# A fused transformer layer on one core: another order of the software-pipelined stages

## What is computed

```
patches: 13 x 13 cells, 11 x 11 of them -> emb = patches @ W.T + b + pos       (121 x 192)
h = concat([emb, txt])                                                          (249 x 192)
h = h + attn(layernorm(h))     # 12 heads of 16, weights and activations rounded to 8 bits,
                               # log_int_softmax: integer exponential, quantised to powers of two
h = h + ffn(layernorm(h))      # 16 experts of 192 -> 128 -> 192 and one shared expert;
                               # router: softmax, best 4 of 8 pairs, best 4 of 16 experts
```

## Time and profile before

| | us |
|---|---|
| median of 3 runs | 3519.49 (3519.41 to 3520.33) |
| the profiled execution's own time | 3518.62 |
| its span | 3516.8 |
| TensorE matmul busy | 3381.6 (96%), 30764 instructions |
| VectorE busy | 3368.5 (96%), 10279 instructions |
| ScalarE busy | 3153.6 (90%), 6228 instructions |
| GpSimd busy | 806.2 (23%), 1647 instructions |

### The profile page before, as it was taken

One profiled execution on the slowest core, in us unless ns is written; L12 is line 12 of the kernel. 1 busy time (PEld: TensorE's weight loads), 2 busy tenths in 40 slices (PEclk: granted clock), 3 DMA queues, 4 the chain that ended last, 5 costly groups with the idle time before them and its releaser, 6 DMA issues.

```text
span 3516.8 us, 98077 instructions
## 1 busy us (share of the span) xinstructions
PE 3381.6 (96%) x30764; PEld 2898.6 (82%) x30764; DVE 3368.5 (96%) x10279; ACT 3153.6 (90%) x6228; POOL 806.2 (23%) x1647
## 2 busy tenths in 40 slices
PE   1589999999999999999999999999999999999999
PEld 1368888888888888888888888888888888888888
DVE  6699999999999999999999999999999999999995
ACT  2799999999999999999999999999999999999992
POOL 3222222222222222222221221222222222222210
PEclk9789999999999999999999999999999999999999
DMA  5101001000000000000000110100000000000000
GB/s 125 27 14 25 25 16 26 25 20 23 25 20 23 24 22 21 24 23 20 25 24 18 25 25 16 26 25 17 25 25 20 23 25 21 22 24 23 20 10 8
DMA packets 157123, 85.77 MB, mean 24 GB/s; under 512 B 51451, under 2 KB 154370, under 8 KB 156610
## 3 DMA queue, kind: packets, MB, share of 16 engines
q1 hardware_dynamic: 153692, 78.82, 9.0%
q10 hardware_dynamic: 2918, 0.67, 0.1%
HBM read 54.89 MB, written 12.24 MB: 19 GB/s over the span
## 4 chain that ended last, share of the span: by engine, by line
PE 92%; DVE 1%; issue 1%; ACT 0%; POOLq 0%; DVEq 0%; POOL 0%
PE pU L1183 33%; PE pY L1209 20%; PE pX L1075 5%; PE pX L1132 5%; PE pS L1120 4%; PE pS L1111 4%; PE pS L1121 4%; PE pX L1094 3%; PE pW L1195 3%; PE pO L1142 2%; PE pY L1192 1%; PE pX L1102 1%; PE pX L1088 1%; PE pX L1151 1%; PE pX L1082 1%
## 5 line engine op out<-in xcount | busy, mean ns | idle before, releaser
L1183 PE MATMUL pU<-x2T,UG 128*128 128x250 f16 x8704 | 1231.6, 270 | 1.0 <-ACT work L676 0.9
L1183 PEld LDWEIGHTS pU<-x2T,UG 128*128 128x128 f16 x8704 | 823.0, 97 | 108.7 <-ACT work L676 1.5
L1209 PE MATMUL pY<-WD,work 128*128 128x192 f32 (+1 forms) x4352 | 810.0, 328 | 0.0
L1209 PEld LDWEIGHTS pY<-WD,work 128*128 128x128 f32 (+1 forms) x4352 | 690.8, 187 | 3.9
L962 DVE SCALAR_TENSOR_TENSOR work<-work,cst 128x249 f32<-128x249 f32 (+1 forms) x1536 | 658.6, 484 | 8.4 <-issue 4.3
L623 ACT ACTIVATE work<-work,alpha 128x249 f32<-128x249 f32 (+1 forms) x1536 | 648.3, 509 | 15.2 <-DVE alpha L974 14.0
L607 ACT ACTIVATE work<-a,room 128x249 bf16<-128x249 int8 (+1 forms) x1536 | 648.3, 514 | 0.0
L1183 PE MATMUL pU<-x2T,UGB 67*128 67x250 f16 x2176 | 592.4, 272 | 0.0
L942 DVE TENSOR_REDUCE rmax<-a 128x4 f32<-128x996 int8 (+1 forms) x384 | 452.9, 1179 | 40.9 <-ACT a L598 40.9
L632 ACT ACTIVATE passing<-pX,cst 128x512 int16<-128x512 int16 (+3 forms) x768 | 480.8, 687 | 6.9 <-PE pX L1132 3.5
L598 ACT ACTIVATE a<-pS,cst 128x996 int8<-128x996 f32 (+1 forms) x384 | 421.4, 1097 | 70.3 <-PE pS L1111 70.1
(11 more groups left out here) (209 smaller groups left out, 5337.5 us busy)
## 6 DMA issues: line engine op xcount, KB each, us to landing
img<-in_x_dram SPq DMA_DIRECT2D x896, 23.5 KB
img<-in_x_dram SPq DMA_DIRECT2D x768, 21.4 KB
qz<-qb SPq DMA_DIRECT2D x768, 15.6 KB, 1.8
h<-in_txt_dram SPq DMA_DIRECT2D x64, 96.0 KB, 2.0
out_dram<-yout SPq DMA_DIRECT2D x64, 96.0 KB
out_dram<-yout SPq DMA_DIRECT2D x64, 90.8 KB
WD<-in_L_ffn_Wd_dram SPq DMA_DIRECT2D x1, 1536.0 KB, 7.6
work<-in_L_ffn_Wu_dram SPq DMA_DIRECT2D x2, 512.0 KB, 6.6
```

What stands on the lines that cost most here:

```text
L1183: a = mm(pU[:, s, q * EVEN:(q + 1) * EVEN], weights, x2T[i % 2][0:w, m, 0:EVEN], start=m == 0, stop=m == BLOCKS - 1)
L1209: a = mm(pY[0:n, t * 256:t * 256 + D], (act_[k % 2] if k else up[0])[:, c:c + n], WD[:, e, :], start=k == 0 and t == 0, stop=e == E - 1, s ...
```

## The change

The list ORDER is replaced. Both lists hold the same 254 (stage, k), and the loop, the waits and every instruction are the same. The new list came out of a search over a table of durations and exclusions in which two more of VectorE's small stages exclude GpSimd; the table itself is not in the kernel. The new list starts at another point of the cycle, so that 167 entries have a shift that is larger by one and 87 the same shift as before; there are 69 steps before and after. Within the cycle the order is new on every engine: of VectorE's 103 neighbouring pairs of stages 6 are kept, of TensorE's 74 there are 9, of ScalarE's 54 there are 8 and of GpSimd's 17 there are 7. SyncE's order is qzload 0, qzload 1, imgload, qzload 2, store, txtload after, and qzload 2, txtload, store, imgload, qzload 0, qzload 1 before.

```diff
         ORDER = [
-            ("r_score", -4, -1), ("low", -3, 4), ("mmG", -5, 7), ("r_biased", -4, -1), ("weigh", -3, 3),
-            ("qkq", -2, 5), ("turnp", -3, 3), ("alpha", -3, 5), ("conv", -2, 2), ("r_pairs", -4, -1),
-            ("down", -5, 5), ("top", -2, 0), ("act", -5, 6), ("gate", -5, 7), ("grow", -3, 4),
...
-            ("value", -2, 1), ("gate", -4, 6), ("share", -2, 4), ("outq", -2, 0), ("turnp", -2, 2),
-            ("copyp", -2, 2), ("pick", -4, 6), ("score", -1, 0), ("qzload", -1, 1), ("grow", -2, 3),
-            ("mmU", -4, 8), ("qk", -1, 5), ("quant", -1, 0),
+            ("below", -2, 5), ("qk", -1, 0), ("pick", -4, 3), ("qkq", -1, 0), ("mmG", -4, 4), ("expo", -2, 3),
+            ("quot", -2, 4), ("below_max", -3, -1), ("qk", -1, 1), ("down", -4, 2), ("u", -2, 4), ("qk", -1, 2),
+            ("silu", -4, 5), ("qkq", -1, 1), ("sum", -2, 2), ("grow", -2, 0), ("alpha", -2, 2),
+            ("share", -2, 2), ("gate", -4, 4), ("weigh", -2, 0), ("mmG", -4, 5), ("sum", -2, 3),
+            ("grow", -2, 1), ("act", -4, 3), ("pick", -4, 4), ("qkq", -1, 2), ("square", -2, 4),
+            ("quot", -2, 5), ("power", -2, 4), ("qk", -1, 3), ("qkq", -1, 3), ("mmU", -4, 6), ("gate", -4, 5),
+            ("weigh", -2, 1), ("low", -2, 2), ("gates", -3, -1), ("act", -4, 4), ("qk", -1, 4), ("qkq", -1, 4),
+            ("mmG", -4, 6), ("r_ratio", -3, -1), ("turnp", -2, 0), ("power", -2, 5), ("pick", -4, 5),
+            ("alpha", -2, 3), ("silu", -4, 6), ("conv", -1, 0), ("down", -4, 3), ("expo", -2, 4),
+            ("gate", -4, 6), ("share", -2, 3), ("act", -4, 5), ("qzload", -1, 0), ("u", -2, 5), ("sum", -2, 4),
+            ("copyp", -2, 0), ("mmU", -4, 7), ("square", -2, 5), ("alpha", -2, 4), ("qk", -1, 5),
+            ("silu", -4, 7), ("conv", -1, 1), ("grow", -2, 2), ("pick", -4, 6), ("score", -1, 0),
+            ("low", -2, 3), ("expo", -2, 5), ("down", -4, 4), ("grow", -2, 3), ("r_exp", -3, -1),
+            ("qkq", -1, 5), ("score", -1, 1), ("conv", -1, 2), ("quant", -1, 0), ("top", -1, 0), ("mmG", -4, 7),
+            ("sum", -2, 5), ("share", -2, 4), ("turnp", -2, 1), ("peak", -1, 0), ("gate", -4, 7),
+            ("qzload", -1, 1), ("weigh", -2, 2), ("imgload", 0, -1), ("quant", -1, 1), ("weigh", -2, 3),
+            ("top", -1, 1), ("mmU", -4, 8), ("r_sum", -3, -1), ("copyp", -2, 1), ("alpha", -2, 5),
+            ("score", -1, 2), ("act", -4, 6), ("below", -1, 0), ("quot", -1, 0), ("low", -2, 4),
+            ("peak", -1, 1), ("r_inverse", -3, -1), ("down", -4, 5), ("mmG", -4, 8), ("value", -2, 0),
+            ("turnp", -2, 2), ("pick", -4, 7), ("silu", -4, 8), ("gate", -4, 8), ("r_score", -3, -1),
+            ("quant", -1, 2), ("top", -1, 2), ("value", -2, 1), ("u", -1, 0), ("share", -2, 5), ("grow", -2, 4),
+            ("mmU", -3, 0), ("square", -1, 0), ("down", -4, 6), ("mmG", -3, 0), ("r_biased", -3, -1),
+            ("copyp", -2, 2), ("weigh", -2, 4), ("low", -2, 5), ("score", -1, 3), ("outq", -2, 0),
+            ("silu", -3, 0), ("turnp", -2, 3), ("mmU", -3, 1), ("act", -4, 7), ("r_pairs", -3, -1),
+            ("pick", -4, 8), ("gate", -3, 0), ("grow", -2, 5), ("below", -1, 1), ("quot", -1, 1),
+            ("power", -1, 0), ("power", -1, 1), ("down", -4, 7), ("r_top_pairs", -3, -1), ("turnp", -2, 4),
+            ("copyp", -2, 3), ("quant", -1, 3), ("act", -4, 8), ("value", -2, 2), ("copyp", -2, 4),
+            ("value", -2, 3), ("expo", -1, 0), ("r_take_pairs", -3, -1), ("u", -1, 1), ("outq", -2, 1),
+            ("down", -4, 8), ("weigh", -2, 5), ("top", -1, 3), ("square", -1, 1), ("r_penalty", -3, -1),
+            ("result", -4, -1), ("r_masked", -3, -1), ("turnp", -2, 5), ("copyp", -2, 5), ("silu", -3, 1),
+            ("mmG", -3, 1), ("value", -2, 4), ("outcast", -2, 0), ("value", -2, 5), ("v", -1, -1),
+            ("sum", -1, 0), ("qzload", -1, 2), ("expo", -1, 1), ("down", -3, 0), ("outq", -2, 2),
+            ("outcast", -2, 1), ("score", -1, 4), ("vq", -1, -1), ("peak", -1, 2), ("below", -1, 2),
+            ("outcast", -2, 2), ("peak", -1, 3), ("r_top", -3, -1), ("alpha", -1, 0), ("project", -2, -1),
+            ("sum", -1, 1), ("share", -1, 0), ("quant", -1, 4), ("mmU", -3, 2), ("r_take", -3, -1),
+            ("quot", -1, 2), ("silu", -3, 2), ("prq", -2, -1), ("residual", -2, -1), ("alpha", -1, 1),
+            ("embed", 0, -1), ("r_weight", -3, -1), ("below", -1, 3), ("stats2", -2, -1), ("score", -1, 5),
+            ("low", -1, 0), ("mean2", -2, -1), ("power", -1, 2), ("r_part0", -3, -1), ("share", -1, 1),
+            ("spread2", -2, -1), ("r_rest", -3, -1), ("gate", -3, 1), ("store", -5, -1), ("mmG", -3, 2),
+            ("r_part1", -3, -1), ("norm2", -2, -1), ("embed_h", 0, -1), ("r_part2", -3, -1), ("quant", -1, 5),
+            ("txtload", 0, -1), ("stats", 0, -1), ("mean", 0, -1), ("split2", -2, -1), ("top", -1, 4),
+            ("chosen", -3, -1), ("spread", 0, -1), ("top", -1, 5), ("mmU", -3, 3), ("copyw", -3, -1),
+            ("turn2", -2, 0), ("u", -1, 2), ("norm", 0, -1), ("quot", -1, 3), ("peak", -1, 4), ("silu", -3, 3),
+            ("split", 0, -1), ("pick", -3, 1), ("vconv", -1, -1), ("gate", -3, 2), ("turn2", -2, 1),
+            ("copy2", -2, 0), ("square", -1, 2), ("copy2", -2, 1), ("low", -1, 1), ("mmU", -3, 4),
+            ("route", -2, -1), ("u", -1, 3), ("act", -3, 1), ("logit", -2, -1), ("below", -1, 4),
+            ("pick", -3, 2), ("turn", 0, 0), ("expo", -1, 2), ("peak", -1, 5), ("mmG", -3, 3), ("copy", 0, 0),
+            ("turn", 0, 1), ("down", -3, 1), ("power", -1, 3), ("silu", -3, 4), ("square", -1, 3),
+            ("lmax", -2, -1), ("copy", 0, 1), ("act", -3, 2), ("mmU", -3, 5), ("gate", -3, 3),
         ]
```

More of the change, by code:

```diff
@@ L304, in fused_layer @@
         ORDER = [
-            ("r_score", -4, -1), ("low", -3, 4), ("mmG", -5, 7), ("r_biased", -4, -1), ("weigh", -3, 3),
-            ("qkq", -2, 5), ("turnp", -3, 3), ("alpha", -3, 5), ("conv", -2, 2), ("r_pairs", -4, -1),
-            ("down", -5, 5), ("top", -2, 0), ("act", -5, 6), ("gate", -5, 7), ("grow", -3, 4),
-            ("r_top_pairs", -4, -1), ("peak", -2, 0), ("score", -2, 1), ("share", -3, 5), ("silu", -5, 8),
-            ("copyp", -3, 3), ("value", -3, 2), ("pick", -5, 7), ("outcast", -3, 0), ("quant", -2, 1),
@@ L310, in fused_layer @@
[L310 to L343, removed]
-            ("r_ratio", -3, -1), ("mmU", -4, 6), ("qk", -1, 4), ("pick", -4, 4), ("quot", -2, 5),
@@ L345, in fused_layer @@
-            ("square", -2, 4), ("u", -2, 5), ("turnp", -2, 0), ("qkq", -1, 3), ("low", -2, 2), ("expo", -2, 4),
-            ("gate", -4, 5), ("silu", -4, 6), ("mmU", -4, 7), ("qkq", -1, 4), ("share", -2, 3),
-            ("r_exp", -3, -1), ("down", -4, 3), ("copyp", -2, 0), ("silu", -4, 7), ("sum", -2, 4),
-            ("r_sum", -3, -1), ("act", -4, 4), ("square", -2, 5), ("r_inverse", -3, -1), ("grow", -2, 2),
-            ("alpha", -2, 4), ("low", -2, 3), ("turnp", -2, 1), ("pick", -4, 5), ("down", -4, 4),
@@ L350, in fused_layer @@
-            ("conv", -1, 0), ("qzload", -1, 0), ("conv", -1, 1), ("power", -2, 5), ("weigh", -2, 2),
-            ("expo", -2, 5), ("value", -2, 0), ("mmG", -4, 6), ("copyp", -2, 1), ("act", -4, 5), ("sum", -2, 5),
-            ("value", -2, 1), ("gate", -4, 6), ("share", -2, 4), ("outq", -2, 0), ("turnp", -2, 2),
-            ("copyp", -2, 2), ("pick", -4, 6), ("score", -1, 0), ("qzload", -1, 1), ("grow", -2, 3),
-            ("mmU", -4, 8), ("qk", -1, 5), ("quant", -1, 0),
+            ("below", -2, 5), ("qk", -1, 0), ("pick", -4, 3), ("qkq", -1, 0), ("mmG", -4, 4), ("expo", -2, 3),
```

## The result

The changed kernel takes 3538.68 us (median of 5 runs, 3538.27 to 3539.97) against 3519.49 (5 runs, 3518.78 to 3520.33): a ratio of 1.0055, 95% interval 1.0041 to 1.0070. It is slower, by 19 us; the two profiled executions, 3539.97 and 3518.62, are 21 apart. The prediction was 3530 and slower. The sign holds, and so does the mechanism: the wait before `vq` is gone, and GpSimd's casts take more from VectorE than that wait was worth. But the period grew by 0.44 us where 0.18 was forecast, and two of the three casts that cost it were not where the prediction had them.

The account below looks back on a forecast made before the run. VectorE's own list was taken to set the 52.23 us period; the parts sum to +0.18 us per image, times 60 is +11 on the profiled 3518.6, making 3529.6, so 3530 us; range 3498 to 3548.

Parts of the forecast that it names:

- 1: VectorE at `vq`: its wait for TensorE's last matmul of `v` goes away, -0.41 us per image.
- 2: VectorE's small stages right behind their own producers: some pairs go, others come, sum 0, bounds -0.1 and +0.1 us per image.
- part 5: VectorE's `norm2` waits for GpSimd's `spread2`, as less work lies between `mean2` and `norm2`: +0.15 us per image.
- 3: `quot` 5 on VectorE now stands behind `act` 3 and no longer behind `r_ratio`: +0.09 us per image.
- 4: GpSimd's casts against VectorE's `expo`: `conv` 2 in `expo` 5 +0.25, smaller ones +0.1 us per image; bounds 0 and +0.6.
- 6: TensorE needs 0.3 to 0.5 us less than 52.2 per image, off the path; transfers cost nothing.
- 7: Fill and drain, before the first result and after the last full step: +3 and -3 us, sum 0, bounds -5 and +5.
- case "3520 to 3540": The forecast itself for the whole kernel: slower, 3520 to 3540 us; chance 0.42.
- rival A: Faster: GpSimd's casts miss `expo` 5 and `norm2` waits only 0.05; -0.27 us per image, 3503 us; chance 0.33.
- B: No change: TensorE sets the period at 52.2 us, 3519.5 us give or take 6; chance 0.17.
- C: Slower by more: a tight loop (`turnp` 5 to `vq`, `mmG` 5 to `gate` 5, `norm2` to `norm`) 0.3 late, 3548 us; chance 0.06.
- D: Whole instructions exclude each other: two casts in `expo` 5 cost 0.40 us each, not 0.12; 3564 us; chance 0.02.

Follow-up runs that it names:

- e3: Changed kernel with `alpha` 1 put between `prq` and `residual`, and `r_part0` in front of `power` 2; 3539.12 us.
- e6: Kernel of e5 with `quot` 5 behind `r_ratio`, `power` 5 behind `alpha` 3 and `alpha` 1 between `prq` and `residual`; 3546.82 us.
- e5: Changed kernel with `vconv` behind `peak` 3, `conv` 2 behind `peak` 0 and `top` 1 in front of `weigh` 2; 3506.16 us.
- e2: Changed kernel with only `vconv` moved earlier, behind `peak` 3 instead of behind `split`; 3518.07 us.
- e8: Kernel before with `lmax` moved behind `expo` 2 and `vconv` put late, behind `peak` 5; 3522.69 us.
- e4: Kernel before with only `vconv` moved later, behind `peak` 5; 3519.46 us.
- e9: Kernel of e5 with `alpha` 1 also put between `prq` and `residual`; 3505.20 us.

## Why the prediction was right, and where its sizes were not

By its own parts, forecast and measured, in us per image:

1. The wait of `vq`: -0.41, measured -0.41 (-0.38 in the mean). Right, and there is no idle time before `vq` in the new trace.
2. Small stages behind their producers: 0, measured -0.07, within the bounds: +0.02 by the table, and `r_part1`, which no longer stands before its reader, costs 0.09 less, which the wait of part 5 hides. e3 adds that the pair `r_part0`, `r_rest` costs nothing at all, because it covers that wait.
3. `quot` 5: +0.09, measured +0.09; e6 shows the reverse.
4. The casts: +0.35, measured +0.67, over the bound of 0.6. This is the step that was mis-sized. `conv` 2 into `expo` 5 was right in place, and nearly in size (0.25, measured 0.29); with some luck, for both the cast and `expo` 5 come half a us later behind `weigh` 5 than I had them (34.9 and 34.5, forecast 34.4 and 33.9). The "smaller ones" were not small: I wrote that `vconv` "now ends as `expo` 2 begins". It starts there, and costs 0.23. GpSimd's subtraction in `split` takes 1.39 in the new order and 0.92 in the old, since it is issued 0.04 behind `low` 1, and `vconv` stands behind it. And `outcast` 2, which I put into `expo` 1, hurt nothing, while `outcast` 1, which I left out, fell on `weigh` 5 (+0.15). I had looked for costs only among `expo` parts, because the earlier trace rows show only those.
5. `norm2` behind `spread2`: +0.15, measured 0.15. `r_part1` takes 0.24 to the start of `norm2`, where by the rule of recorded time less 0.08 it would cost 0.09; the row in the table shows only +0.06 because `r_part1` paid 0.09 before for its place in front of `r_part2`. The power took 0.71 and met no `quot`, and from `mean2` to `norm2` it is 1.62, as reckoned for a `spread2` that is not held up (1.6). The profile shows no idle time there, so the sign that I named, idle time before line 932, did not come; the wait has to be read from the starts.
6. TensorE off the path: right. It lost 2.2 us of its 400, in 0.3 us waits for `weigh` 5. But my count that it needs 0.3 to 0.5 less than 52.2 is not borne out: in e5, at 52.12, it is busy 399.82 of 400, so that no run shows this room. The transfers: nothing, as said.
7. Fill and drain: 0 forecast, -5.3 measured (-3.1 and -2.2), just outside the bound of -5.

The sum, -0.41 - 0.07 + 0.09 + 0.67 + 0.15 = +0.43, times 60 is +26, less 5 is the +21 between the profiled executions, where +11 was forecast. Part 4 alone was 19 us short; parts 2 and 7 were out by 4 and 5 us the other way, which is luck.

How much the sign owes to luck is seen with `conv` 2 alone in part 4: -0.41 - 0.07 + 0.09 + 0.29 + 0.15 = +0.05, 3 us, and less 5 for fill and drain no change at all. e2, in which `vconv` and `outcast` 1 cost VectorE nothing, is nearly that case, and it took 3518.07. The loss comes from two collisions of which the prediction had one as a near miss (`vconv` and `expo` 2) and the other not at all (`outcast` 1 and `weigh` 5), with 0.1 for all the smaller ones. And 3538.7 lies at the upper end of the case "3520 to 3540", in a range that took in rival A as well.

The rivals.

- A (3503) is near what e5 shows: with GpSimd out of the way the new order gives 3506. That a mere shift of the engines by some tenths would have done the same is likely, but was not shown.
- B named a floor of 52.2 for TensorE; e5 goes to 52.12 with TensorE at 399.82 of 400, so the floor is there or lower.
- C did not occur in the changed kernel, but e6 makes its loop at `gate` 5.
- D asked for 0.40 from each cast in `expo` 5, and 0.17 and 0.12 came. A cast issued together with a VectorE instruction delays it by 0.17 (0.40 cast, `expo` 5), 0.22 (0.41, `weigh` 5), 0.25 (0.40, `power` 5 of e6) and 0.30 (0.52, `expo` 2 of e8), not by 0.40 to 0.52.

The starts say why. In these rows the one that waits seems to begin its own work some 0.14 before the recorded end of the first (0.21 before it, where the one that waits is an `expo` part): `weigh` 5 ends 0.68 after the cast was issued, and 0.68 is 0.41 + 0.41 - 0.14. An estimate from these rows is then: the price is the recorded time of the one issued first, less 0.14 to 0.21, less the distance between the two starts. The 0.14 is from `weigh` 5 and the 0.21 from `expo` 5; with them it gives 0.25 for `power` 5 of e6 (measured 0.25), 0.30 for `expo` 2 of e8 (0.30), 0.49 for the subtraction behind `low` 1 (0.47), 0.08 for `r_pairs` of e5 (0.07) and nothing for e4. My 0.12 from the earlier trace rows was of casts issued 0.06 and 0.30 into a part, which wait themselves first; it is the lowest case, and I used it for all.

The page SBUF — State Buffer of the Trainium skill, in "Who interferes with whom", says that the instruction issued first keeps the shared ports for its whole length. The rows above agree with it in who goes first and, with the 0.14 to 0.21 taken off a recorded time, in how long; what failed in D was to take the recorded time itself as the price.

What is open: the changed kernel's neighbours in the last rows of the table (`sum` 4, `r_part2`) were not tried alone; that `low` 1 is what lengthens `split` was read from its place in the trace only, in all 57 images; and whether VectorE or TensorE holds the period of e5 and e9.
